# Six more edge groups on the binned path, and the last block's bins added up two pairs per step

## What is computed

```python
h = jnp.maximum(_layernorm(x, axis=-1), 0.0)          # 6250 x 64
m = jnp.concatenate([h[dst], edge_attr], axis=1)      # 206250 x 128
m = relu(m @ W1.T + b1)
m = relu(m @ W2.T + b2)                               # 206250 x 128
agg = segment_sum(m, src, 6250) / maximum(count, 1)   # sum by the unsorted index
z = relu(concatenate([h, agg, u[0]], axis=1) @ Wa.T + ba)
out = x + z @ Wb.T + bb                               # 6250 x 64
```

## Time and profile before

| | before |
|---|---|
| median of 3 runs | 2166.95 us |
| profiled execution | 2171.31 us |
| its span | 2169.6 us |
| granted TensorE clock, mean | 0.937 |
| PE busy | 1828.7 us (84%) |
| DVE busy | 1555.7 us (72%) |
| ACT busy | 743.1 us (34%) |
| POOL busy | 1713.9 us (79%) |
| scatters L719 and L707 | 876 and 184 |

### The profile page before, as it was taken

One profiled execution on the slowest core, in us unless ns is written; L12 is line 12 of the kernel. 1 busy time (PEld: TensorE's weight loads), 2 busy tenths in 40 slices (PEclk: granted clock), 3 DMA queues, 4 the chain that ended last, 5 costly groups with the idle time before them and its releaser, 6 DMA issues.

```text
span 2169.6 us, 44519 instructions
## 1 busy us (share of the span) xinstructions
PE 1828.7 (84%) x12535; PEld 1545.1 (71%) x12535; DVE 1555.7 (72%) x5312; ACT 743.1 (34%) x1779; POOL 1713.9 (79%) x1100
## 2 busy tenths in 40 slices
PE   3798888898999899998989999899899997677717
PEld 2576766787787787777777787788787886566615
DVE  8876666777777787777777787777777886455418
ACT  3243433333334343333333443333333332111103
POOL 5288888888888888888888888888888888888850
PEclk8799999999999999999999999999999999788859
DMA  7798888999999999998999999999999999687756
GB/s 282 225 181 165 160 158 158 186 203 201 200 197 195 195 205 207 199 208 176 207 195 196 202 196 204 205 193 198 202 195 208 202 218 198 92 140 129 112 109 187
DMA packets 395312, 406.30 MB, mean 187 GB/s; under 512 B 51933, under 2 KB 294269, under 8 KB 394557
## 3 DMA queue, kind: packets, MB, share of 16 engines
q1 hardware_dynamic: 241164, 332.21, 53.9%
q0 software_dynamic: 152640, 70.08, 34.3%
q10 hardware_dynamic: 1264, 1.11, 0.2%
HBM read 226.75 MB, written 176.44 MB: 186 GB/s over the span
## 4 chain that ended last, share of the span: by engine, by line
POOL 63%; issue 25%; DVE 5%; PE 4%; DMA 3%; SPq 1%; ACT 0%; POOLq 0%; ACTq 0%; DVEq 0%
POOL sums L719 49%; POOL sums L707 13%; DMA sums<-regA,idx 2%; PE bank L1142 1%; PE bank L1166 1%; PE bank L1120 1%; DVE regC L1020 1%; DVE regC L890 1%; DVE regC L1031 1%; DVE regC L896 0%; DMA regC<-in_src_cols 0%; PE bank L1156 0%; DVE regC L1021 0%; DVE regC L1022 0%; DVE regC L901 0%
## 5 line engine op out<-in xcount | busy, mean ns | idle before, releaser
L719 POOL DMA_INDIRECT sums<-regA,idx x876 | 1385.7, 1582 | 321.0 <-issue 263.5
L999 DVE TENSOR_TENSOR h<-bank,b2n 128x512 f32<-128x512 f32 x403 | 278.8, 692 | 419.9 <-PE bank L1166 283.3
L1120 PEld LDWEIGHTS bank<-h,regC 128*128 128x128 f32 x2944 | 385.7, 201 | 239.8 <-issue 223.1
L1120 PE MATMUL bank<-h,regC 128*128 128x130 f32 x2944 | 420.9, 288 | 120.6 <-ACT h L811 78.6
L1166 PE MATMUL bank<-w,h 128*128 128x128 f32 x3224 | 454.5, 287 | 0.0
L1142 PE MATMUL bank<-regA,L 128*128 128x512 f32 x806 | 422.0, 606 | 2.6 <-DVE regA L940 2.0
L1166 PEld LDWEIGHTS bank<-w,h 128*128 128x128 f32 x3224 | 420.7, 204 | 1.1 <-ACT h L796 0.6
L790 ACT ACTIVATE regC<-bank 128x260 f32<-128x260 f32 x736 | 285.3, 388 | 256.9 <-PE bank L1120 148.1
L1156 PEld LDWEIGHTS bank<-h,regC 128*128 128x128 f32 x1752 | 239.1, 200 | 188.0 <-issue 184.6
L804 ACT ACTIVATE regA<-bank 128x516 f32<-128x516 f32 x219 | 131.7, 601 | 690.6 <-DMA sums<-regA,idx 589.6
L796 ACT ACTIVATE h<-bank 128x512 f32<-128x512 f32 x403 | 240.1, 596 | 306.3 <-PE bank L1142 187.4
(11 more groups left out here) (130 smaller groups left out, 1223.9 us busy)
## 6 DMA issues: line engine op xcount, KB each, us to landing
regC<-slots SPq DMA_DIRECT2D x245, 260.0 KB
regA<-in_ea SPq DMA_DIRECT2D x202, 256.0 KB
slots<-regC SPq DMA_DIRECT2D x184, 260.0 KB
slots<-regC SPq DMA_DIRECT2D x184, 203.1 KB
src<-rows_src SPq DMA_DIRECT2D x219, 128.0 KB
dstR<-rows_dst SPq DMA_DIRECT2D x403, 64.0 KB
sums<-regA,idx POOLq DMA_INDIRECT x876
sums<-zeros SPq DMA_DIRECT2D x20, 645.0 KB, 8.4
```

Of the source, the lines that this page charges most:

```text
L719: nc.gpsimd.indirect_dma_start(out=sums[k], out_offset=bass.IndirectOffsetOnAxis(ap=idx[:, n % RING, t:t + 1], axis=0), in_=scat[:, n % 4, ...
L999: VE.tensor_tensor(h2[:, g % 2, :, 0:H], psL2(g % 2).rearrange("p (t f) -> p t f", t=TPG), b2n[:, :].unsqueeze(1).broadcast_to([P, TPG, H] ...
L1120: last = T.matmul(psSlot(t)[:, k, :], place, h2[:, g % 2, t, :], start=True, stop=True)
```

## The change

Binned groups now run to 381 (190 in place of 184; the last block has 30 groups, and 213 groups stay plain in place of 219). The last block's units begin at step 390 and go two per step, to step 402, where one is left. The buffers of unit rows (`BR`) are three in place of two; SP's wait before a unit is for the unit three before. In the last block the units alternate between two PSUM banks, and PE waits before a unit until the one two before has been added. The one-hot buffers stay two. The units of the fifth block are spread over 60 steps in place of 48. Everything else is as it was.

```diff
-LAST_SORTED = 370
+LAST_SORTED = 382
-UNIT_RING = 2
+UNIT_RING = 3
+TAIL = 2
 def unit_steps():
     firsts = [block[-1] + VREAD + 2 for block in BLOCKS]
     for k in range(len(BLOCKS)):
         for q in range(UNITS):
-            span = firsts[k + 1] - firsts[k] if k + 1 < len(BLOCKS) else UNITS
-            even = 2 if span >= 2 * UNITS else 1
-            s = firsts[k] + even * (span * q // (even * UNITS))
+            if k + 1 < len(BLOCKS):
+                span = firsts[k + 1] - firsts[k]
+                s = firsts[k] + 2 * (span * q // (2 * UNITS))
+            else:
+                s = firsts[k] + q // TAIL
             at.setdefault(s, []).append((k, q))
...
+TAIL_UNIT = len(UNIT_NO) - UNITS
+def added_for(m):
+    return m if m <= TAIL_UNIT else m - 1
...
-        psUnit = bank[:, 1, 0:PAIR * C]
+        def psUnit(m):
+            return bank[:, 0 if m >= TAIL_UNIT and m % 2 else 1, 0:PAIR * C]
...
-                summed_bins = psUnit[:, 0:nb * C].rearrange("p (b c) -> p b c", c=C)
+                summed_bins = psUnit(m)[:, 0:nb * C].rearrange("p (b c) -> p b c", c=C)
...
                 pe.wait_ge(oh2_ready, m + 1)
-                wait(pe, acc_ready, m)
+                wait(pe, acc_ready, added_for(m))
                 for i in range(nb):
                     for t in range(TPG):
-                        last = T.matmul(psUnit[:, i * C:(i + 1) * C], oh2[0:rows, m % 2, i, t, :] if not general else zeros[0:rows, 0:LO],
+                        last = T.matmul(psUnit(m)[:, i * C:(i + 1) * C], oh2[0:rows, m % 2, i, t, :] if not general else zeros[0:rows, 0:LO],
                                         BR[0:rows, m % UNIT_RING, i, t, 0:C], start=t == 0, stop=t == TPG - 1)
                 last.then_inc(unit_done, 1)
```

More of the change, by code:

```diff
@@ L136 @@
 assert LO * NBIN == NKEPT >= N and P < SLOTS <= PW and NG + max(VSUM, VLAG) < STEPS and LAST_SORTED <= 2 * ODD
-assert NBIN == BA * BA and PACK * BA <= P and NS % (4 * PACK) == 0 and max(len(u) for u in UNITS_AT.values()) == 1
+assert NBIN == BA * BA and PACK * BA <= P and NS % (4 * PACK) == 0 and all(len(UNITS_AT[s]) == 1 for s in UNITS_AT if UNITS_AT[s][0][0] < len(BLOCKS) - 1)
 def build(nc, x, src_cols, dst_cols, src_rows, dst_rows, ea, u, w1t, b1, w2t, b2, wat, ba, wbt, bb, out):
```

## The result

The changed kernel takes 2171.9 us (median of 20 runs, 2168.0 to 2177.4), the kernel before in the same sessions 2167.2 (20 runs, 2161.7 to 2170.4): a ratio of 1.0024, interval 1.0015 to 1.0032. It is slower by some 5 us.

The account below looks back on a forecast made before the run. POOL's issuing of scatters was taken as the bound. Six more binned groups save 33.9 us, but the last block's loops use that up and 11.3 more: 2166.95 + 11.3 = 2178.3 us, range 2150 to 2196.

Parts of the forecast that it names:

- part 2: Steps 390 to 402, two units (a, then b) per step: a loop of 14.0 us per step against POOL's 7.5.
- the start of the loops: Step 390, after group 383's last scatter lands: PE takes 5.4 us, so its first unit, a(390), is done at 1926.3.
- the eleven loops: From a(390) to a(401), the first units of steps 390 and 401: eleven loops of 14.0 us, ending at 2080.3.
- the last step: Step 402, one unit of one bin: the same loop, 10.4 + 2.0 us, then group 401's sums, 2.0, and ACT's copy, 0.6.
- Part 1: Six more binned groups, 371 to 381: 18 scatters less, 33.9 us off POOL, their added work priced at nothing.
- The loop and its links: Last block, once per step: a done, b's transfers, dstR and src issued and landed, masks, add, next a; 14.0 us.
- 10.4 us to the add: In each loop, from SP's issue of the unit's transfers to the end of DVE's add: 10.4 us.
- Unit a cold (at the slow clock), 3.6 us: PE, idle some 5 us in each loop, runs the step's first unit in 3.6 us, against 1.95 at full clock.
- rival B: PE is at 2.4 GHz when unit a starts, 1.95 us in place of 3.6: step 12.4, time 2158; chance 0.18.
- break-even of 13.1: Length of a step in the last block's loop, 13.1 us, at which the change would neither gain nor lose.
- Rival A: The loop in the last block hides behind POOL's 7.5 us per step, the whole 33.9 stands: 2133; chance 0.15.
- Rival C: Transfers land sooner in the last block as POOL starves and queues empty: step 13.4, time 2171; chance 0.12.

Follow-up runs that it names:

- part 1 alone: The kernel before with only the binned groups extended to 381, the last block's units still one per step: 2147.6 us, ratio 0.990.
- SP's order: The changed kernel with the last block's unit transfers issued one SP step later, behind the next step's dstR and src: 2160.9 us, ratio 0.996.
- four buffers: The changed kernel with four buffers of unit rows in place of three, nothing else: 2135.5 us, ratio 0.9841.
- adds first: The changed kernel with DVE's adds of the last block's units put first in its step, ahead of L952 and the masks: 2133.5 us, ratio 0.9839.
- part 2 alone: The changed kernel with binned groups only to 369 as before, last block's units still two per step with three buffers and two banks: 2208.1 us, ratio 1.0189.

## Why the prediction was right and wrong

The mechanism, the sign and the place were right; the size was not: +11.3 us forecast, 4.7 us measured (the medians' difference, and that of the two traces from group 370 on). Three terms of the sum of part 2 were too large: the start of the loops (2.6 us), the eleven loops (1.7) and the last step (2.8). In the first two the path was right and a size was off; in the last step the path itself was wrong.

- *Part 1, 33.9 us off POOL, at no cost.* Right: 56.0 us from group 370 to 382, where the sum had 56.5, and part 1 alone keeps POOL full.
- *The loop and its links.* Right: in the trace, unit b's data, `dstR`, `src`, masks, add, unit a, in this order and with the last arrival from `src`. Taking the `src` link out (SP's order), the add out of its shadow (adds first), or the wait itself one unit back (four buffers) shortened the step each time.
- *10.4 us to the add.* Near: 10.2, as 13.85 less 3.6 for unit a. The larger transfers, priced at 0 to 0.6, cost nothing that shows; `src` landed 3.4 to 4.4 us after its issue, 3.8 on average over the eleven loops.
- *Unit a cold (at the slow clock), 3.6 us.* Right: 3.5 to 3.8 in ten of the loops and 2.7 in the first, 3.6 on average, so rival B falls. Its price decides the sign all the same: at 1.95 us, as in the warm kernel with four buffers, the step would be 12.2 us, under the break-even of 13.1 (an estimate from these rows).
- *Eleven loops of 14.0.* 152.3 us in place of 154: 1.7 us too much, all of it in the 10.4.
- *a(390) done 79.5 us after group 370 starts.* It was 76.9, so 2.6 us too much. I had given PE the slow clock in step 390, 5.4 us, from a step in which it had been idle for 3.8 us. Here it had been idle for 2.8, and took 3.8 us from the sums to the end of unit a, its first row being the one below: 1.6 us of the 2.6. The rest is that group 383's last scatter started 68.9 us after group 370, not 69.7, and landed in 3.4 us, not 3.6. (The parts as I wrote them give 1926.1 and not 1926.3.)

```profile
1911.85 1.13 PE L1168 MATMUL bank<-h,regC 128*128 128x129 f32 x8 [2.78 <-ACT regA L816]
```

- *The last step, 12.4 us and then the sums of group 401.* This is the step that failed in its path, and the largest of the three. I gave step 402 the same loop. But DVE's `dstR` and `src` are those of the group after, and group 403 does not exist; nor does step 402 have a unit b, and the one bin of a(402) had been issued at 2059.45. Nothing had to be fetched between a(401) and a(402). PE's row below ends unit a(402) 5.4 us after a(401) (2068.0), where the sum had 12.4:

```profile
2072.30 1.06 PE L1143 MATMUL bank<-regC 120*128 120x129 f32 x8
```

So not unit a(402) but the copy of group 400's sums set the end: POOL starts that group at 2072.99 and goes through 401 and 402 without a pause. From a(401) to group 402's first scatter it is 19.8 us; the sum had 22.6. 2.8 us too much.

The three add up to 7.1 us, on 256.1 forecast and 249.0 measured between the first scatters of groups 370 and 402. The forecast was the small difference of two large terms, 33.9 us gained and 45.2 lost, so 7.1 us too much in the second, 16% of it, made the forecast more than twice the result. By the same sum 0.9 us less in each loop (14.0 to 13.1) would have turned the sign: the range (2150 to 2196) had to be as wide as it was. Rival A (hidden) needed 10.2 us a step, and the kernel with adds first shows that point to be about right. Rival C came true in part. I had named `src` landing under 4 us as its sign, and that is so in eight of the eleven loops; but in the trace of before the same landing took 3.6 to 4.8 us in the nine times that DVE waited for it between 1890 and 2060 us, 4.2 on average, and was under 4 in three of them. The 4.74 us of the row I followed lies near the upper end. So `src` came 0.4 us sooner, and the stretch to the add was 10.2 us, between my 10.4 and the 9.8 of rival C. Of the tests named ahead, the pairs of transfers, the idle times before each group (5.7 to 7.2 us, from group 395) and the waits for `src` came out; that POOL would stay full to group 393 was right to within one group.

## What to carry to other kernels

A wait in an in-order queue is paid by everything queued behind it: before two pieces of work go where one was, draw the loop through each wait and count how many steps it spans. Here three buffers at two units per step reach one and a half steps back where two buffers at one unit reached two, so a loop that had closed every second step closed every step; one buffer more, or the consumer's add ahead of the late arrivals, gave back the whole gain. In a sum over a repeated loop, the first and the last turn are written out by themselves: here they made 5.4 of the 7.1 us of error.

## What the hardware showed that was not expected

With 31 groups in a block (252 KB per transfer) the data of a unit, two transfers, lands some 20 us after that of the unit before; with 30 (244 KB) it is there 5.4 us after the unit that it had to wait for; in the kernel with 32 (260 KB) nobody waits for it. A count of 29 is as slow as 31 (2518.7 and 2531.5 us for the kernel, against 2135.5 with 30). One group more in the last block cost 396 us, and padding the transfer by one group of zeros took them back.

The same stretch of the same work can take several microseconds more in one execution than in another: the kernel of part 2 alone and the one with only a third buffer do the same up to group 360, and reach it at 1792.47 and 1796.14 us. For a change of 5 us the traces say where the time goes, and only the 20 runs say that there is one.
